# Two maxima over all partitions per group: by one PE product with the identity and a VectorE maximum, in place of GpSimd

## The reference, cut to what matters

```python
def _quantize_activations_groupwise(x):
    n = x.shape[0]
    gs = n // NUM_GROUPS            # 32 // 5 = 6 images
    xq = jnp.zeros_like(x)
    for g in range(NUM_GROUPS):     # 5 groups, the last 2 images stay 0
        ag = x[g * gs:(g + 1) * gs]
        gamma = jnp.max(jnp.abs(ag))
        xq = xq.at[g * gs:(g + 1) * gs].set(jnp.clip(ag * QB / (gamma + EPS), -QB + EPS, QB - EPS))
    return xq

def _bitlinear(x, W, b):
    Wb = _binarize_weights_groupwise(W)
    y = jnp.einsum('btc,oc->bto', x, Wb) + b
    return _quantize_activations_groupwise(y)

h = _bitlinear(x, W1, b1)                   # 192 -> 768
h = jax.nn.gelu(h, approximate=False)
out = _bitlinear(h, W2, b2)                 # 768 -> 192
```

## Time and profile before

| | |
|---|---|
| Median of 3 runs | 4434.95 us (4434.21 to 4440.96) |
| The profiled execution | 4435.83 us, its span 4434.0 us |
| PE busy | 3979.8 us, 90% of the span |
| DVE busy | 3055.0 us, 69% |
| ACT busy | 2969.4 us, 67% |
| POOL (GpSimd) busy | 363.8 us, 8% |
| Granted TensorE clock, mean | 0.979 |
| Chain that ended last | PE 67%, DVE 13%, issue 11%, ACT 5%, POOL 1% |

### The profile page before, as it was taken

One profiled execution on the slowest core, in us unless ns is written; L12 is line 12 of the kernel. 1 busy time (PEld: TensorE's weight loads), 2 busy tenths in 40 slices (PEclk: granted clock), 3 DMA queues, 4 the chain that ended last, 5 costly groups with the idle time before them and its releaser, 6 DMA issues.

```text
span 4434.0 us, 114786 instructions
## 1 busy us (share of the span) xinstructions
PE 3979.8 (90%) x39240; PEld 2906.6 (66%) x39240; DVE 3055.0 (69%) x5559; ACT 2969.4 (67%) x6669; POOL 363.8 (8%) x375
## 2 busy tenths in 40 slices
PE   5999999879999898999999879999898999999888
PEld 4777774667777646777774667777646777774666
DVE  5666776766666677666766766666677666766776
ACT  2777776667776655777776667776655777776666
POOL 1000002000000110000002000000110000002000
PEclk8999999999999999999999999999999999999999
DMA  3111111011211101111111011211101111111011
GB/s 74 37 37 38 43 37 29 0 51 43 57 41 37 37 0 44 37 37 44 38 37 29 0 51 44 57 40 37 37 0 44 37 37 44 37 37 29 0 44 44
DMA packets 48832, 161.01 MB, mean 36 GB/s; under 512 B 12612, under 2 KB 13126, under 8 KB 48198
## 3 DMA queue, kind: packets, MB, share of 16 engines
q1 hardware_dynamic: 48326, 154.40, 14.5%
HBM read 28.52 MB, written 25.17 MB: 12 GB/s over the span
## 4 chain that ended last, share of the span: by engine, by line
PE 67%; DVE 13%; issue 11%; ACT 5%; POOL 1%; DMA 1%; DVEq 1%; ACTq 1%; SPq 0%; POOLq 0%
PE PT L698 12%; PE OUT L718 10%; PE S L684 7%; DVE nmax L1231 5%; PE PT L824 5%; PE S L743 5%; PE S L794 3%; PE S L642 3%; PE FR L642 3%; PE FR L586 2%; DVE work L385 2%; ACT work L952 1%; PE FR L649 1%; DVE XT L1100 1%; PE S L686 1%
## 5 line engine op out<-in xcount | busy, mean ns | idle before, releaser
L1231 DVE TENSOR_REDUCE nmax<-S 128x1 f32<-128x384 f32 (+7 forms) x1536 | 1147.7, 754 | 885.2 <-PE S L686 872.3
L952 ACT ACTIVATE work<-S,nmax 128x384 f32<-128x384 f32 (+7 forms) x1536 | 1137.0, 741 | 534.6 <-DVE nmax L1231 525.0
L698 PE MATMUL PT<-ident,work 128*128 128x128 f32 x6912 | 1068.9, 278 | 90.1 <-DVE work L385 59.6
L698 PEld LDWEIGHTS PT<-ident,work 128*128 128x128 f32 x6912 | 745.3, 142 | 242.5 <-ACT work L952 53.9
L385 DVE COPY work<-PT 128x512 f32<-128x512 f32 x768 | 524.4, 683 | 34.5 <-PE PT L698 27.5
L944 ACT ACTIVATE work<-PT 128x384 f32<-128x384 f32 (+3 forms) x768 | 335.9, 437 | 143.5 <-PE PT L698 131.8
L684 PE MATMUL S<-KS,QS 128*128 128x512 f16 (+3 forms) x1152 | 321.5, 334 | 99.5 <-ACT work L952 66.7
L684 PE MATMUL S<-odd 128*128 128x512 f16 (+3 forms) x1152 | 315.9, 329 | 59.9 <-ACT work L952 58.7
L686 PE MATMUL S<-causal,identb 128*128 128x128 bf16 x1536 | 339.0, 221 | 0.0
L956 ACT ACTIVATE work<-PT 128x128 f32<-128x128 f32 (+3 forms) x768 | 332.1, 432 | 1.4 <-PE PT L698 1.2
L743 PE MATMUL S<-odd,W1b 128*128 (+1 forms) x1080 | 259.6, 393 | 49.5 <-ACT work L995 41.2
(11 more groups left out here) (209 smaller groups left out, 6008.8 us busy)
## 6 DMA issues: line engine op xcount, KB each, us to landing
X<-in_x SPq DMA_DIRECT2D x32, 768.0 KB, 5.3
odd<-hi_z SPq DMA_DIRECT2D x128, 192.0 KB, 4.2
odd<-odd SPq DMA_DIRECT2D x128, 192.0 KB, 4.3
out_y<-work SPq DMA_DIRECT2D x64, 384.0 KB, 3.7
QS<-hi_z SPq DMA_DIRECT2D x64, 192.0 KB, 4.1
QS<-odd SPq DMA_DIRECT2D x64, 192.0 KB, 4.1
KS<-hi_z SPq DMA_DIRECT2D x64, 192.0 KB, 4.3
KS<-odd SPq DMA_DIRECT2D x64, 192.0 KB, 4.5
```

The lines of the kernel that those rows point to most:

```text
L698: last = tr(bank[:, P * (j - c0):P * (j - c0) + P], PS[m % 2][:, m // 2 % 2, P * j:P * j + P], ident[:, :])
L952: A(PS[n % 2][:, n // 2 % 2, 0:w], S[:, n % 2, 0:w], ACT.Exp, bias=nmax[:, n % MAXES:n % MAXES + 1], accum_out=rowsum[:, sum_col(n):sum_co ...
L1231: v.tensor_reduce(nmax[:, n % MAXES:n % MAXES + 1], S[:, n % 2, 0:P * (qtile(n) + 1)], AX.X, ALU.max, negate=True).then_inc(max_made, 1)
```

## The change

GpSimd's two reductions go. In their place PE multiplies: its weights are the column `run` of 128 values, read 128 times over (`broadcast_to`), its moving operand is the f32 identity. So row m, column n of the result is the sum over k of run[k] * I[k, n], which is run[n]: every partition of the bank FR then holds all 128 values side by side, and a DVE maximum along the columns gives every partition the maximum of all.

```diff
@@ gpsimd, group_tail
-                pool.wait_ge(max1_step, (g + 1) * (GS * MH + 1) + MH)
-                alone(pool)
-                pool.partition_all_reduce(gam1, run1, P, RMAX).then_inc(gam1_made, 1)
-
-                pool.wait_ge(max2_step, (g + 1) * (GS * 2 + 1))
-                alone(pool)
-                pool.partition_all_reduce(gam2, run2, P, RMAX).then_inc(gam2_made, 1)
@@ tensor, group_tail, between y1 and y
-                pe.wait_ge(max1_step, nb * (GS * MH) + g + MH)
+                def spread_to_all(run, made):
+
+                    mm(FR[:, 0:P], run.broadcast_to([P, P]), ident[:, :], start=True, stop=True).then_inc(made, 1)
+
+                pe.wait_ge(max1_step, nb * (GS * MH + 1) + MH)
                 alone(pe)
+                spread_to_all(run1, gam1_made)
@@ tensor, group_tail, behind the last y2
                 y2(ab, 1)
+                pe.wait_ge(max2_step, nb * (GS * 2 + 1))
+                alone(pe)
+                spread_to_all(run2, gam2_made)
@@ scalar
-                act.wait_ge(quant1_step, (g + 1) * 4)
+                act.wait_ge(quant1_step, (g + 1) * 5)
@@ vector, the first maximum
                 dve.wait_ge(gam1_made, nb)
-                q0 = g * 4
-                v.tensor_scalar(ge, gam1, Q_EPS, None, ALU.add).then_inc(quant1_step, 1)
+                alone(dve)
+                q0 = g * 5
+                v.tensor_reduce(gam1, FR[:, 0:P], AX.X, ALU.max).then_inc(quant1_step, 1)
                 dve.wait_ge(quant1_step, q0 + 1)
+                v.tensor_scalar(ge, gam1, Q_EPS, None, ALU.add).then_inc(quant1_step, 1)
+                dve.wait_ge(quant1_step, q0 + 2)
                 v.reciprocal(gr, ge).then_inc(quant1_step, 1)
...
@@ vector, the second maximum
                 dve.wait_ge(gam2_made, nb)
-                q0 = g * 5
-                v.tensor_scalar(ge2, gam2, Q_EPS, None, ALU.add).then_inc(quant2_step, 1)
+                alone(dve)
+                q0 = g * 6
+                v.tensor_reduce(gam2, FR[:, 0:P], AX.X, ALU.max).then_inc(quant2_step, 1)
                 dve.wait_ge(quant2_step, q0 + 1)
+                v.tensor_scalar(ge2, gam2, Q_EPS, None, ALU.add).then_inc(quant2_step, 1)
...
```

More of the change, by code:

```diff
@@ L1285, in group_tail @@
                 dve.wait_ge(gam1_made, nb)
-                q0 = g * 4
+                alone(dve)
+                q0 = g * 5
+                v.tensor_reduce(gam1, FR[:, 0:P], AX.X, ALU.max).then_inc(quant1_step, 1)
+                dve.wait_ge(quant1_step, q0 + 1)
                 v.tensor_scalar(ge, gam1, Q_EPS, None, ALU.add).then_inc(quant1_step, 1)
-                dve.wait_ge(quant1_step, q0 + 1)
+                dve.wait_ge(quant1_step, q0 + 2)
                 v.reciprocal(gr, ge).then_inc(quant1_step, 1)
-                dve.wait_ge(quant1_step, q0 + 2)
+                dve.wait_ge(quant1_step, q0 + 3)
                 v.tensor_scalar(r1, gr, QB, None, ALU.mult).then_inc(quant1_step, 1)
-                dve.wait_ge(quant1_step, q0 + 3)
+                dve.wait_ge(quant1_step, q0 + 4)
                 v.tensor_scalar(rb1, B1[:, :], r1, None, ALU.mult).then_inc(quant1_step, 1)
@@ L1345, in group_tail @@
                 dve.wait_ge(gam2_made, nb)
-                q0 = g * 5
+                alone(dve)
+                q0 = g * 6
+                v.tensor_reduce(gam2, FR[:, 0:P], AX.X, ALU.max).then_inc(quant2_step, 1)
+                dve.wait_ge(quant2_step, q0 + 1)
                 v.tensor_scalar(ge2, gam2, Q_EPS, None, ALU.add).then_inc(quant2_step, 1)
-                dve.wait_ge(quant2_step, q0 + 1)
+                dve.wait_ge(quant2_step, q0 + 2)
                 v.reciprocal(gr2, ge2).then_inc(quant2_step, 1)
@@ L1351, in group_tail @@
                 v.tensor_scalar(c2n, ge2, -(QB - Q_EPS) / QB, None, ALU.mult).then_inc(quant2_step, 1)
-                dve.wait_ge(quant2_step, q0 + 4)
+                dve.wait_ge(quant2_step, q0 + 5)
                 v.tensor_scalar(r2, gr2, QB, None, ALU.mult).then_inc(quant2_step, 1)
-                dve.wait_ge(quant2_step, q0 + 5)
+                dve.wait_ge(quant2_step, q0 + 6)
                 alone(dve)
```

## The result

| | before | changed |
|---|---|---|
| Median of the runs | 4437.27 us (4434.21 to 4440.96, 4 runs) | 4411.49 us (4408.27 to 4412.92, 4 runs) |
| Ratio to before | 1 | 0.9943, 95% interval 0.9931 to 0.9954 |
| The profiled execution, its span | 4435.83, 4434.0 us | 4412.92, 4411.1 us |
| POOL busy | 363.8 us | 359.3 us |
| Mean granted TensorE clock | 0.979 | 0.982 |

A forecast was written before the change was run, and what follows sets the result against it. The whole core stands waiting for GpSimd's first maximum, which follows a configuration switch. 32.1 + 3.0 - 10.8 + 3.1 = 27.4 us off the profiled 4435.83 gives 4408.4, a median of 4407.5 us, range 4402 to 4415.

The forecast's parts named there:

- The stall: First maximum, after the reduction over 36 columns: DVE's five waits on GpSimd, 32.1 us, all exposed, would go.
- The pair: PE product plus DVE maximum replacing each reduction: 1.08 us each, ten times 10.8 us; bounds 0.8 to 1.5 each.
- The second place: Second maximum, after the reduction over 12 columns: 0.60 us becomes 1.08, losing 0.48 us each, 2.4 us in all.
- The clock: TensorE clock no longer falls before L824, which then starts 7.8 us after the first GELU in all groups: 3.1 us back.
- The periods: Sign of success: each group's period would be 825 to 827 us.
- The moved products: Next stage's first 12 PE products start some 0.5 us later, stay covered; PE then idles about 0.9 us, not 6.55.
- The sum: All terms at both maxima and the clock: 27.4 us gained, bounds 20 to 31 us.
- Dear pairs: Rival: clock still falls or each pair takes up to 1.5 us; gain 20 to 24 us, 4411 to 4415; chance 0.14.
- More back at the second place: Rival: new product keeps the clock up, output turning done some 1 us sooner per group, 4401 to 4404; chance 0.07.
- Not what it says: Rival: the first wait's 5.8 us belong to another thing and stay; about 4440 us; chance 0.04.
- Slower by the clock: Rival: 0.9 us of PE idle time starts a clock fall in the stage's dense part; 4454 us; chance 0.03.

The follow-up runs named there:

- early switch: Kernel before, plus one unneeded GpSimd reduction over partitions behind the group's last layer-norm step, where GpSimd is idle: 4405.78 us, ratio 0.9929.
- first maximum alone: Changed kernel with the second maximum put back as a GpSimd reduction, only the first made on PE: 4436.76 us, 1.0001 of the kernel before.
- kept-warm kernel: Kernel before, plus 24 further PE products per group filling PE's idle time in the wait for the first maximum: 4435.64 us, ratio 1.0002.
- product behind the 12: Changed kernel with the first maximum's product queued behind PE's 12 products made ahead instead of ahead of them: 4426.93 us, ratio 0.9962 to the kernel before.

## Why the prediction was right

**The stall** was right in place, size and cause: 32.1 us of waits, gone; the early switch and the first maximum alone show that it is the configuration switch, and that it falls on the first reduction after elementwise work, wherever that stands.

**The pair** was forecast at 1.08 us and is 1.08 from the reduction's end to the next small instruction (782.04 to 783.12 in the first group). Two of its terms were off and cancel: the hop from DVE to PE is 0.15 us, not 0.28, and the product 0.46, not 0.05 + 0.278. I had priced it from a turning (L698's 0.278 us), which is one pass; an f32 product is two. That the two cancel is luck.

**The second place** loses 0.49 us per group, forecast 0.48. **The clock** gives back 3.1 us, forecast 3.1, and the kept-warm kernel shows it without the change. But that L824 is late in three groups of five was read from one trace; in the second one of before it is two groups and 2.0 us. The periods are 826.0 to 826.2 us in the first trace of the changed kernel, 823.5 to 826.4 over all three, forecast 825 to 827. **The moved products** stay covered: 1.08 us of idle time in place of the 0.9 forecast.

**The sum** of the two places is 27.4 us against 27.4. The median is 4411.5 and not 4407.5 because of what no term held: the base of three runs stood 2.3 us low (4434.95 against 4437.27 in the result, 4436 to 4439 elsewhere), and the gain by the medians is 25.8 us and not 27.4 (23.6 on the other chip). The clock's term can account for 1.1 us of that; the remainder lies in the rest, which moves by more than that from one trace to the next.

**The rivals.** Dear pairs: no, 1.08 us. More back at the second place: no; there the turning of the output starts 2.33 us after DVE's first piece in all groups of all kernels, though with the first maximum alone the clock is at half there from 884 to about 897 us, twice as long as before, so DVE sets the pace. Not what it says: no, the switches are gone from the group loop. Slower by the clock: not in any group, since the 1.08 us of idle time bring no fall; the product behind the 12 shows such a fall, with 3.67 us, in four groups of five.

By the Trainium skill's rule that names GpSimd for a reduction over partitions ("GPSIMD Engine Reference", section "Engine selection") both reductions would have stayed. The trace bears the rule out, but only with the switch out of the way, as in the early switch; as the kernel stood, it was wrong for the pair of them. And to move the first reduction only, which the prediction held possible in the same place, gains nothing here: the first maximum alone stands at 1.0001 of the time before.

## What to carry to other kernels

A small operation's price is in the list of waits, not in its busy time: 0.38 us of reduction cost 6.4. Where GpSimd switches its configuration for a kind of operation that it runs seldom (the MODIFY_POOL_CONFIG records), look for idle time ahead of it and call it there once for nothing; here that beat moving the work to faster engines, and cost one line. Where a stall of the whole core goes, read the clock behind it as well.

## What the runs showed of the hardware

- GpSimd's switch from elementwise work to the reduction over partitions: 5.6 to 6.3 us from what it waits for to its start, in every trace that has these reductions in the loop, against 0.2 us without a switch. It is paid in each of the five groups. The profile shows no DMA packet in it (778.6 to 784.6 us of before) and not what GpSimd does in it. The switch back lies in idle time in the loop; at the start of the program, in the trace of before, 6.7 us lie between the end of a reduction and the next elementwise step (L495), put down to "issue".
- The reduction itself answers in 0.6 us from DVE to DVE, less than one PE product and one DVE maximum (1.08 us), and less than a turning and a maximum (0.92).
- The f32 product of 128 x 128 x 128 is two weight loads of 0.187 us and two passes, 0.46 us in all; a turning of the same size one load of 0.133 and one pass of 0.295.
- The granted clock falls at the end of the attention in 53 of the 65 stretches of the thirteen traces, and two executions of one kernel differ by 4.4 us with it before the 714th microsecond. A difference of 0.1% between two single traces of this kernel says nothing unless it is read place by place.
